# Turning gathered embedding rows on VectorE instead of TensorE, for five of sixteen groups, in a DLRM interaction kernel

## The chip, the cores and the metric

One core of a Trainium2 chip runs the whole kernel. The metric is the device time of one execution in microseconds, and the median over the runs counts.

## What is computed

The batch has 512 samples. For each sample the 26 embedding rows (128 float32 numbers each) of 26 tables and the dense row of 128 numbers are put together as 27 vectors; the 351 products of two different vectors follow, and then a tower of three layers:

```python
combined = jnp.concatenate([dense_features[:, None, :], sparse_features], axis=1)
interactions = jnp.einsum('bnd,bmd->bnm', combined, combined)
interactions_flat = interactions[:, _TRIU_I, _TRIU_J]
z = jnp.concatenate([dense_features, interactions_flat], axis=1)
h = jnp.concatenate([z, r_dense_features], axis=1)
h = jnp.maximum(h @ W_top1 + b_top1, 0.0)     # 607 -> 512
h = jnp.maximum(h @ W_top2 + b_top2, 0.0)     # 512 -> 256
y = h @ W_top3                                # 256 -> 1
```

All data is float32.

## The kernel before, in words

The features' buffer `xt` (line 140) holds the 27 vectors with the feature dimension on the partitions: partition d, then pair of samples, then vector, then sample within the pair. It is filled in three ways.

The dense vector is copied by ScalarE. Eleven small tables (1,000 rows) are not gathered. They are loaded whole, and `lookup` (line 314) multiplies them on TensorE with one-hot matrices that VectorE makes (`compare`, line 551). A table enters as a rounded high part, which ScalarE casts, and a low part, which VectorE subtracts (`make_low`, line 567). ScalarE copies the result from PSUM into `xt`. There are 13 lookups: tables 0 to 8 over the whole batch, tables 9 and 10 over one half of the batch each time. Lookups 11 and 12 serve the second half, and TensorE mixes them with the first products.

The other fifteen tables are gathered by GpSimd with indirect DMAs (line 307), one for each table and tile of 128 samples, so 60 in all. A gathered block `rows_sb` (line 139) has samples on the partitions and must be turned. The blocks are worked on in groups: each of the four tiles has four groups, of 4, 4, 4 and 3 blocks. So groups 0 to 3 belong to tile 0, 4 to 7 to tile 1, 8 to 11 to tile 2 and 12 to 15 to tile 3. `turn_group(g)` (line 340) transposes a group's blocks on TensorE into one of the two banks of `ps_rows`, and `copy_group(g)` (line 657) on ScalarE takes the bank to `xt`. `rows_sb` has room for two tiles, so the gathers of group g from 8 on wait until group g-8 has been turned (line 300).

Once all of a tile's vectors are in `xt`, `gram(t, quarter)` (line 353) makes 32 products of 27 by 27 numbers for each of its four quarters. On VectorE, `pack(t)` (line 583) transposes them from PSUM in blocks of 32 by 32 (line 589) and copies the upper triangle with nine copies (line 594) into `z`. `turn_z` on TensorE and `copy_z` on ScalarE turn `z` for layer 1 (`layer1_dense`, `layer1_pairs`), whose results go through `relu1_low` on ScalarE and `relu1_high` on VectorE (line 602) to `layer2`, `relu2` and `layer3`. The tiles are pipelined: TensorE puts the products of tile t+1 between the layer parts of tile t, in an order that is written out by hand (lines 471 to 542). The order on VectorE and ScalarE is written out too (lines 614 to 621 and 699 to 746). Each engine runs its own list in order and waits on semaphores.

At the places that matter here, TensorE runs (line 474) group 7 behind lookup 10, (line 484) group 8, `layer1_dense(0, ...)`, `turn_z(0)`, group 9, `gram(1, 0)`, the pairs of tile 0 with the rest of tile 1's products, `layer2(0, 0)`, `gram(1, 3)`, `layer2(0, 1)`, `layer1_dense(1, ...)`, (line 501) group 10, `turn_z(1)`, group 11 and `gram(2, 0)`. The same round follows for tile 1, with (line 517) group 12, `turn_z(2)`, group 13, `layer1_pairs(2, 0)`, group 14, group 15 and the products of tile 3. VectorE, after its work for the lookups, runs `pack(0)`, `relu1_high(0)`, `pack(1)`, `relu1_high(1)` and so on.

Of the kernel before, what the change touches and what calls it, by code (L numbers as in the profile page):

```python
# [15 lines left out]
P = 128  # L16
B = 512
D = 128
# [3 lines left out]
RUN = 2  # L22
TILES = B // P
# [38 lines left out]
ROWS_RING = 2  # L62
# [4 lines left out]
FIRST_HALF_UP_TO = NOH  # L67
# [3 lines left out]
FIRST_GATHERED = 1 + NOH  # L71
GROUP_SIZES = [4, 4, 4, 3]
GROUP_STARTS = [sum(GROUP_SIZES[:i]) for i in range(len(GROUP_SIZES))]
GROUPS = [(t, i, k) for t in range(TILES) for i, k in zip(GROUP_STARTS, GROUP_SIZES)]
assert sum(GROUP_SIZES) == len(GATHERED)

AFTER_LOOKUP = [[], [], [], [0], [1], [2], [3], [4], [5], [6], [7]]
LOOKED_UP_BESIDE = sum(len(gs) for gs in AFTER_LOOKUP)
assert sum(AFTER_LOOKUP, []) == list(range(LOOKED_UP_BESIDE)) and len(AFTER_LOOKUP) == FIRST_HALF_UP_TO
GROUPS_UP_TO = [sum(t <= tile for t, _, _ in GROUPS) for tile in range(TILES)]  # L80

WARM_UP = 13
GATHERS_PER_LOOKUP = 3
# [38 lines left out]
def build(nc, dense_by_column, ids, ids_by_table, tables, w1, w2, columns, identity, out):  # L122
    with ExitStack() as ctx:
        def sb(name, shape, dt):
            return ctx.enter_context(nc.sbuf_tensor(name, shape, dt))

        def sem(name):
            return ctx.enter_context(nc.semaphore(name))
# [10 lines left out]
        rows_sb = sb("rows_sb", [P, ROWS_RING, len(GATHERED), D], F32)  # L139
        xt = sb("xt", [P, B // RUN, N, RUN], F32)  # L140
# [21 lines left out]
        def bank(name, banks=1):  # L162
            return ctx.enter_context(nc.psum_tensor(name, [P, banks, BANK], F32))

        ps_a = bank("ps_a", 2)
        ps_rows = bank("ps_rows", 2)
# [14 lines left out]
        group_landed = [sem(f"group_landed{g}") for g in range(len(GROUPS))]  # L181
# [9 lines left out]
        lookup_copied = sem("lookup_copied")  # L191
        group_turned = sem("group_turned")
        group_copied = sem("group_copied")
        gram_done = sem("gram_done")
        blocks_turned = sem("blocks_turned")
        triangle_packed = sem("triangle_packed")
# [27 lines left out]
        def h1_block(t, m):  # L224

            return ps_a[:, m // 2, (m % 2) * P:(m % 2 + 1) * P]
# [61 lines left out]
        @block.gpsimd  # L288
        def _(pool):

            for c in SIZES:
                first = FIRST_COLUMN[c]
                pool.iota(row_id[:, first:first + c], [[1, c]], base=0, channel_multiplier=c,
                          allow_small_or_imprecise_dtypes=True).then_inc(row_id_ready, 1)
                pool.iota(row_id[:, first + c:first + c + 1], [[1, 1]], base=1 - c, channel_multiplier=-c,
                          allow_small_or_imprecise_dtypes=True).then_inc(row_id_ready, 1)
            pool.wait_ge(ids_landed, 16)
            for g, (t, first, n) in enumerate(GROUPS):
                if t >= ROWS_RING:
                    pool.wait_ge(group_turned, g - ROWS_RING * len(GROUP_SIZES) + 1)  # L300
                for k in range(first, first + n):
                    f = GATHERED[k]
                    issued = t * len(GATHERED) + k
                    if issued >= GATHERS_AHEAD and (issued - GATHERS_AHEAD) % GATHERS_PER_LOOKUP == 0:
                        lookups = (issued - GATHERS_AHEAD) // GATHERS_PER_LOOKUP + 1
                        pool.wait_ge(lookup_done, min(lookups, len(LOOKUPS)))
                    pool.indirect_dma_start(  # L307
                        rows_sb[:, t % ROWS_RING, k, :], None, tables[f],
                        bass.IndirectOffsetOnAxis(ids_sb[:, t, f:f + 1], 0),
                    ).then_inc(group_landed[g], 16)  # L310

        @block.tensor
        def _(pe):
# [26 lines left out]
            def turn_group(g):  # L340

                t, first, n = GROUPS[g]
                if g >= 2:
                    pe.wait_ge(group_copied, g - 1)
                if g == 0:
                    pe.wait_ge(ident_landed, 16)
                pe.wait_ge(group_landed[g], 16 * n)
                for slot in range(n):
                    last = pe.transpose(ps_rows[:, g % 2, slot * P:(slot + 1) * P],  # L349
                                        rows_sb[:, t % ROWS_RING, first + slot, :], ident)  # L350
                last.then_inc(group_turned, 1)

            def gram(t, quarter):

                half, first = divmod(quarter * SPQ, SPB)
                if quarter == 0:

                    pe.wait_ge(group_copied, GROUPS_UP_TO[t])  # L360
                    pe.wait_ge(lookup_copied, FIRST_HALF_UP_TO if t < TILES // 2 else len(LOOKUPS))
                    if t == 0:
                        pe.wait_ge(dense_copied, 1)
                        pe.wait_ge(gram_zeroed, 1)
                    else:
                        pe.wait_ge(blocks_turned, t)
                for s in range(first, first + SPQ):
                    for j in range(P // NPAD):
                        b = t * P + j * NPAD + half * SPB + s
                        x = xt[:, b // RUN, :, b % RUN]  # L370
                        last = pe.matmul(ps_gram[j * NPAD:j * NPAD + N, half, s * N:(s + 1) * N], x, x,  # L371
                                         start=True, stop=True)
                if quarter == QUARTERS - 1:
                    last.then_inc(gram_done, 1)
# [96 lines left out]
            for i in range(FIRST_HALF_UP_TO):  # L471
                lookup(i)
                for g in AFTER_LOOKUP[i]:
                    turn_group(g)
# [6 lines left out]
            gram(0, 3)  # L481
            lookup(FIRST_HALF_UP_TO + 1, [2, 3])

            turn_group(8)
            layer1_dense(0, 0)
            layer1_dense(0, 1)
            turn_z(0)
            turn_group(9)
            gram(1, 0)
            layer1_pairs(0, 0)  # L490
            layer1_pairs(0, 1)
# [6 lines left out]
            layer2(0, 1)  # L498
            layer1_dense(1, 0)
            layer1_dense(1, 1)  # L500
            turn_group(10)
            turn_z(1)
            turn_group(11)

# [9 lines left out]
            layer2(1, 1)  # L514
            layer1_dense(2, 0)
            layer1_dense(2, 1)
            turn_group(12)
            turn_z(2)
            turn_group(13)

# [24 lines left out]
        def _(dve):  # L545
# [37 lines left out]
            def pack(t):  # L583

                dve.wait_ge(gram_done, t + 1)
                if t:
                    dve.wait_ge(triangle_packed, t)
                blocks = ps_gram[:, :, 0:SPB * N].rearrange("p k (s m) -> p m k s", m=N)
                dve.transpose(zz[:, 0:N, :], blocks).then_inc(blocks_turned, 1)  # L589
                dve.wait_ge(blocks_turned, t + 1)  # L590
                if t:
                    dve.wait_ge(z_turned, t)
                for r, (i, length, at) in enumerate(TRIANGLE):
                    last = dve.tensor_copy(  # L594
                        z[:, at:at + TRI * length].rearrange("p (r l) -> p r l", r=TRI),
                        diagonal(i, length))
                    if t == TILES - 1 and r in CHUNK_ENDS:
                        last.then_inc(last_packed, 1)
                if t < TILES - 1:
                    last.then_inc(triangle_packed, 1)  # L600

            def relu1_high(t):

                dve.wait_ge(h1_done, 2 * (t + 1))
                if t == 0:
                    dve.wait_ge(layers_landed, 32)
                if t >= 2:
                    dve.wait_ge(h2_done, t - 1)
                for m in range(M1 // 2, M1):
                    last = dve.tensor_scalar(h1[:, t % 2, m, :], h1_block(t, m),  # L610
                                             b1_sb[:, m:m + 1], 0.0, ALU.add, ALU.max)
                last.then_inc(h1_high_ready, 1)

            pack(0)
            relu1_high(0)
            pack(1)
            relu1_high(1)
            pack(2)
            relu1_high(2)
# [4 lines left out]
        def _(act):  # L624
# [32 lines left out]
            def copy_group(g):  # L657
                t, first, n = GROUPS[g]
                slots = slice(FIRST_GATHERED + first, FIRST_GATHERED + first + n)
                act.wait_ge(group_turned, g + 1)  # L660
                act.copy(xt[:, t * P // RUN:(t + 1) * P // RUN, slots, :].rearrange("p q n r -> p n q r"),  # L661
                         ps_rows[:, g % 2, 0:n * P].rearrange("p (n q r) -> p n q r", n=n, r=RUN)).then_inc(group_copied, 1)

            def copy_z(t):
                act.wait_ge(z_turned, t + 1)
# [43 lines left out]
            for h in range(FIRST_HALF_UP_TO):  # L709
# [6 lines left out]
                if h == WORK_RING:  # L716
                    act.wait_ge(dense_landed, 16)
                    act.copy(xt[:, :, 0, :], dense_sb[:, :].rearrange("p (q r) -> p q r", r=RUN)).then_inc(dense_copied, 1)
                for g in AFTER_LOOKUP[h]:
                    copy_group(g)  # L720
            copy_lookup(FIRST_HALF_UP_TO)
            copy_lookup(FIRST_HALF_UP_TO + 1)
            copy_group(8)
            copy_z(0)
            copy_group(9)
            relu1_low(0)
            relu2(0)
            copy_group(10)
            copy_z(1)
            copy_group(11)  # L730
            relu1_low(1)
            relu2(1)
            copy_group(12)
            copy_z(2)
            copy_group(13)
            relu1_low(2)
# [41 lines left out]
```

## Time and profile before

| | us |
|---|---|
| median of 3 runs | 103.11 (102.64 to 103.51) |
| the profiled execution's own time | 103.07 |
| its span, first to last instruction | 101.2 |
| TensorE busy in it | 94.3 |
| VectorE busy in it | 52.8 |
| ScalarE busy in it | 48.3 |
| GpSimd busy in it | 60.6 |

The span is what the profile's times count from. The 1.9 us between it and the execution's own time lie before the first and after the last instruction. The granted TensorE clock was 1.0 over the whole span.

### The profile page before, as it was taken

To read this page: it belongs to the slowest core of one execution; us is meant where nothing else is said; L and a number is where in the kernel's file an instruction comes from. 1 tells how busy PE (TensorE), PEld (TensorE's weight loads), DVE (VectorE), ACT (ScalarE), POOL (GpSimd) and SP (SyncE) were. 2 spreads that over 40 slices of the span, in tenths; PEclk is the share of its full clock that TensorE was granted. 3 is DMA by queue.
4 is the path that set the end of the run, shared out by engine and by line. 5 is a ranking of instruction groups with operands and counts; after the bars stand their busy time and mean duration, and the time that the engine had idled before them with its cause. 6 is when DMAs were issued, how large, how long until landed. Compare 5 with 4: busy or idle time off the path is not lost.

```text
span 101.2 us, 3474 instructions
## 1 busy us (share of the span) xinstructions
PE 94.3 (93%) x1525; PEld 77.4 (77%) x1525; DVE 52.8 (52%) x116; ACT 48.3 (48%) x82; POOL 60.6 (60%) x66
## 2 busy tenths in 40 slices
PE   5999997999999999999997999997999989979990
PEld 2357665778888888899986898896898979977870
DVE  4599999999999989907000800243001801035200
ACT  2844998299399489565310342007020356005251
POOL 1488877777777777777777777777777730000000
PEclk9999999999999999999999999999999999999999
DMA  2899999999997999622222222212222220000000
GB/s 61 237 323 262 296 274 279 262 263 278 283 240 209 243 324 369 209 55 52 58 58 52 57 53 58 62 52 58 52 57 53 58 52 0 6 6 0 6 0 1
DMA packets 5365, 13.46 MB, mean 133 GB/s; under 512 B 1731, under 2 KB 1991, under 8 KB 5222
## 3 DMA queue, kind: packets, MB, share of 16 engines
q1 hardware_dynamic: 3260, 9.11, 31.0%
q0 software_dynamic: 1920, 3.94, 15.5%
q8 instruction: 12, 0.20, 0.8%
q10 hardware_dynamic: 170, 0.18, 0.6%
q14 instruction: 3, 0.02, 0.1%
HBM read 13.23 MB, written 0.00 MB: 131 GB/s over the span
## 4 chain that ended last, share of the span: by engine, by line
PE 71%; DVE 18%; DMA 3%; issue 3%; ACT 3%; DVEq 0%
PE ps_a L334 29%; PE ps_gram L371 12%; DVE onehot L562 12%; PE ps_a L420 9%; PE ps_rows L349 6%; PE ps_h L434 5%; DVE part_sb L571 4%; PE ps_a L410 3%; DMA idrow<-ids_by_table 3%; PE ps_a L397 3%; PE ps_rows L447 2%; DVE table_sb L589 1%; ACT xt L661 1%; PE ps_h L460 1%; DVE z L594 1%
## 5 line engine op out<-in xcount | busy, mean ns | idle before, releaser
L307 POOL DMA_INDIRECT rows_sb<-tbl,ids_sb x60 | 60.1, 1002 | 20.8 <-issue 16.8
L334 PE MATMUL ps_a<-onehot,part_sb 125*128 125x512 f32 (+1 forms) x208 | 45.2, 367 | 0.8 <-DVE part_sb L571 0.5
L334 PEld LDWEIGHTS ps_a<-onehot,part_sb 125*128 125x128 f32 x208 | 34.1, 188 | 8.6 <-DVE part_sb L571 2.4
L562 DVE TENSOR_SCALAR onehot<-idrow,row_id 125x1024 fp32r<-125x1024 int16 (+1 forms) x42 | 27.9, 717 | 2.2 <-DMA idrow<-ids_by_table 1.7
L571 DVE TENSOR_TENSOR part_sb<-table_sb,part_sb 125x512 fp32r<-125x512 f32 x22 | 14.4, 677 | 2.3 <-ACT part_sb L633 2.3
L654 ACT COPY xt<-ps_a 128x512 f32<-128x512 f32 (+1 forms) x13 | 7.4, 570 | 16.3 <-PE ps_a L334 16.3
L371 PE MATMUL ps_gram<-xt 128*27 128x27 f32 x1024 | 13.2, 195 | 2.0 <-issue 1.1
L371 PEld LDWEIGHTS ps_gram<-xt 128*27 128x27 f32 x1024 | 11.0, 108 | 4.6 <-issue 1.5
L610 DVE TENSOR_SCALAR table_sb<-ps_a,columns_sb 128x128 f32<-128x128 f32 x8 | 2.4, 347 | 20.9 <-PE ps_a L420 17.8
L589 DVE STREAM_TRANSPOSE table_sb<-ps_gram 128x864 f32<-128x864 f32 x4 | 4.3, 1083 | 16.7 <-issue 8.5
L633 ACT CAST part_sb<-table_sb 125x1024 fp32r<-125x1024 f32 (+1 forms) x12 | 11.6, 975 | 2.7 <-DMA table_sb<-tbl 2.7
L661 ACT COPY xt<-ps_rows 128x512 f32<-128x512 f32 (+1 forms) x16 | 9.8, 613 | 1.8 <-PE ps_rows L349 1.7
L420 PE MATMUL ps_a<-table_sb,w_sb 128*128 128x128 f32 x72 | 9.7, 283 | 0.3 <-ACT table_sb L668 0.3
L691 ACT ACTIVATE table_sb<-ps_h,columns_sb 128x128 f32<-128x128 f32 x6 | 1.9, 363 | 16.9 <-PE ps_h L434 16.9
L349 PE MATMUL ps_rows<-ident_sb,rows_sb 128*128 128x128 f32 x60 | 9.2, 272 | 0.0
L420 PEld LDWEIGHTS ps_a<-table_sb,w_sb 128*128 128x128 f32 x72 | 8.6, 192 | 0.7 <-ACT table_sb L668 0.5
L349 PEld LDWEIGHTS ps_rows<-ident_sb,rows_sb 128*128 128x128 f32 x60 | 7.2, 141 | 0.8
L434 PE MATMUL ps_h<-table_sb,w_sb 128*128 128x128 f32 x48 | 7.0, 288 | 0.0
L643 ACT ACTIVATE distance<-idrow,row_id 125x1024 f32<-125x1024 int16 (+1 forms) x6 | 6.5, 1078 | 0.4 <-DMA idrow<-ids_by_table 0.4
L468 PE MATMUL ps_z<-zeros 128*128 128x512 bf16 x13 | 5.2, 588 | 1.2 <-DVE zeros L546 1.2
L648 ACT ACTIVATE onehot<-distance 125x1024 fp32r<-125x1024 f32 (+1 forms) x6 | 5.9, 991 | 0.4
L684 ACT ACTIVATE table_sb<-ps_a,columns_sb 128x128 f32<-128x128 f32 x8 | 2.5, 364 | 7.4 <-PE ps_a L420 5.4
(35 smaller groups left out, 44.0 us busy)
## 6 DMA issues: line engine op xcount, KB each, us to landing
table_sb<-tbl SPq DMA_DIRECT2D x11, 448.0 KB
idrow<-ids_by_table SPq DMA_DIRECT2D x5, 256.0 KB, 5.7
w_sb<-w SPq DMA_DIRECT2D x1, 1280.0 KB, 8.2
rows_sb<-tbl,ids_sb POOLq DMA_INDIRECT x60, 3.6
table_sb<-tbl SPq DMA_DIRECT2D x10, 52.0 KB
w_sb<-w SPq DMA_DIRECT2D x1, 512.0 KB, 8.8
dense_sb<-dense_by_column SPq DMA_DIRECT2D x1, 256.0 KB, 7.7
idrow<-ids_by_table ACTq DMA_DIRECT2D x1, 128.0 KB, 2.9
```

What stands on the lines that cost most here:

```text
L307: pool.indirect_dma_start(rows_sb[:, t % ROWS_RING, k, :], None, tables[f], bass.IndirectOffsetOnAxis(ids_sb[:, t, f:f + 1], 0),).then_inc ...
L334: last = pe.matmul(ps_a[:, i % 2, a:b], parts_sb[part][:, w, c * D:(c + 1) * D], unit_onehot(u, c)[:, member, a:b], start=(part == HIGH an ...
L349: last = pe.transpose(ps_rows[:, g % 2, slot * P:(slot + 1) * P], rows_sb[:, t % ROWS_RING, first + slot, :], ident)
L371: last = pe.matmul(ps_gram[j * NPAD:j * NPAD + N, half, s * N:(s + 1) * N], x, x, start=True, stop=True)
L420: last = pe.matmul(h1_block(t, m), w1_sb[:, c, m * P:(m + 1) * P], zt[:, t % 2, c, :], start=False, stop=(c == ZC - 1), skip_group_check=True)
L434: last = pe.matmul(h2_block(t, m), w2_sb[:, k, m * P:(m + 1) * P], h1[:, t % 2, k, :], start=(k == 0 and m == 0), stop=(k == M1 - 1), skip ...
L562: dve.tensor_scalar(unit_onehot(u, c), idrow[0:VP, w, 0:n, :], row_id[0:VP, first + c:first + c + 1], None, ALU.is_equal).then_inc(onehot_ ...
L571: dve.tensor_tensor(parts_sb[LOW][:, w, columns], table_sb[0:VP, s, columns], parts_sb[HIGH][:, w, columns].bitcast(F32), ALU.subtract).th ...
L633: act.copy(parts_sb[HIGH][:, w, first:end], table_sb[0:VP, s, first:end]).then_inc(part_ready[HIGH], 1)
L643: act.activation(distance[:, 0:n, :], idrow[0:VP, w, 0:n, :], ACT.Abs, bias=row_id[0:VP, negated:negated + 1]) \
L654: act.copy(xt[:, a // RUN:b // RUN, 1 + h, :], ps_a[:, i % 2, a:b].rearrange("p (q r) -> p q r", r=RUN)).then_inc(lookup_copied, 1)
L661: act.copy(xt[:, t * P // RUN:(t + 1) * P // RUN, slots, :].rearrange("p q n r -> p n q r"), ps_rows[:, g % 2, 0:n * P].rearrange("p (n q ...
```

## The change

Groups 7, 8, 9, 10 and 12 are no longer turned by TensorE and copied by ScalarE. A new function on VectorE, `lay_group`, turns each group with 16 transposes: for each of four bands of 32 samples and each of four bands of 32 features, one instruction turns the group's 4 (or 3) blocks of 32 by 32 from `rows_sb` straight into `xt`. Groups 7 and 8 are laid ahead of `pack(0)`, groups 9 and 10 between `pack(0)` and `relu1_high(0)`, group 12 between `pack(1)` and `relu1_high(1)`. The remaining eleven groups keep their places. Their semaphore values and the choice of the `ps_rows` bank go by the place among the turned groups.

```diff
-AFTER_LOOKUP = [[], [], [], [0], [1], [2], [3], [4], [5], [6], [7]]
+AFTER_LOOKUP = [[], [], [], [0], [1], [2], [3], [4], [5], [6], []]
+LAID = [7, 8, 9, 10, 12]
+TURNED = [g for g in range(len(GROUPS)) if g not in LAID]
+TURNED_UP_TO = [sum(GROUPS[g][0] <= tile for g in TURNED) for tile in range(TILES)]
+LAID_UP_TO = [sum(GROUPS[g][0] <= tile for g in LAID) for tile in range(TILES)]
+BLOCK = 32
...
                 if t >= ROWS_RING:
-                    pool.wait_ge(group_turned, g - ROWS_RING * len(GROUP_SIZES) + 1)
+                    freed = g - ROWS_RING * len(GROUP_SIZES)
+                    if freed in LAID:
+                        pool.wait_ge(group_laid, LAID.index(freed) + 1)
+                    else:
+                        pool.wait_ge(group_turned, TURNED.index(freed) + 1)
...
-                    pe.wait_ge(group_copied, GROUPS_UP_TO[t])
+                    pe.wait_ge(group_copied, TURNED_UP_TO[t])
+                    if LAID_UP_TO[t]:
+                        pe.wait_ge(group_laid, LAID_UP_TO[t])
...
-            turn_group(8)
             layer1_dense(0, 0)
             layer1_dense(0, 1)
             turn_z(0)
-            turn_group(9)
             gram(1, 0)
...
-            turn_group(10)
             turn_z(1)
             turn_group(11)
...
-            turn_group(12)
             turn_z(2)
             turn_group(13)
...
+            def lay_group(g):
+
+                t, first, n = GROUPS[g]
+                slots = slice(FIRST_GATHERED + first, FIRST_GATHERED + first + n)
+                dve.wait_ge(group_landed[g], 16 * n)
+                for a in range(0, P, BLOCK):
+                    samples = slice((t * P + a) // RUN, (t * P + a + BLOCK) // RUN)
+                    for d in range(0, D, BLOCK):
+                        last = dve.transpose(
+                            xt[d:d + BLOCK, samples, slots, :].rearrange("p q n r -> p n q r"),
+                            rows_sb[a:a + BLOCK, t % ROWS_RING, first:first + n, d:d + BLOCK])
+                last.then_inc(group_laid, 1)
+
+            lay_group(7)
+            lay_group(8)
             pack(0)
+            lay_group(9)
+            lay_group(10)
             relu1_high(0)
             pack(1)
+            lay_group(12)
             relu1_high(1)
```

On ScalarE `copy_group(8)`, `(9)`, `(10)` and `(12)` go from the written-out list, and group 7's copy goes with `AFTER_LOOKUP`.

## Rows read from the trace of the kernel before

**Rows 1.** The page: busy time of each engine, share of the span and instructions.
```profile
PE 94.3 (93%) x1525; PEld 77.4 (77%) x1525; DVE 52.8 (52%) x116; ACT 48.3 (48%) x82; POOL 60.6 (60%) x66
```

**Rows 2.** The chain that ended last, in order of time: start us, us, what.
```profile
48.52 0.33 PE ps_rows L349 x3
...
57.08 0.44 PE ps_rows L349 x4
...
57.65 1.13 PE ps_a L410 x8
...
67.03 1.09 PE ps_h L434 x8
...
69.01 0.45 PE ps_rows L349 x4
...
69.49 0.61 ACT xt L661
...
70.47 0.41 ACT xt L661
...
70.92 0.72 PE ps_gram L371 x50
...
81.29 0.49 ACT table_sb L668
...
81.82 1.61 PE ps_a L420 x12
...
84.53 0.33 PE ps_rows L349 x3
```

**Rows 3.** VectorE's timeline from 40 us on: start us, us, instructions, idle before.
```profile
46.78 0.68 DVE L581 TENSOR_TENSOR w1d<-w_sb 128x512 f32<-128x512 f32 x1
...
55.97 1.08 DVE L589 STREAM_TRANSPOSE table_sb<-ps_gram 128x864 f32<-128x864 f32 x1 [8.51 <-issue]
57.09 1.02 DVE L594 COPY z<-table_sb 128x78 f32<-128x78 f32 x9
64.38 0.61 DVE L610 TENSOR_SCALAR table_sb<-ps_a,columns_sb 128x128 f32<-128x128 f32 x2 [6.27 <-PE ps_a L420]
67.08 1.08 DVE L589 STREAM_TRANSPOSE table_sb<-ps_gram 128x864 f32<-128x864 f32 x1 [2.09 <-PE ps_gram L371]
...
75.68 0.61 DVE L610 TENSOR_SCALAR table_sb<-ps_a,columns_sb 128x128 f32<-128x128 f32 x2 [6.46 <-PE ps_a L420]
```

**Rows 4.** Groups of VectorE's instructions by form: busy us, mean ns of one.
```profile
L571 DVE TENSOR_TENSOR part_sb<-table_sb,part_sb 125x512 fp32r<-125x512 f32 x22 | 14.4, 677 | 2.3 <-ACT part_sb L633 2.3
L589 DVE STREAM_TRANSPOSE table_sb<-ps_gram 128x864 f32<-128x864 f32 x4 | 4.3, 1083 | 16.7 <-issue 8.5 <-PE ps_gram L371 8.2
...
L610 DVE TENSOR_SCALAR table_sb<-ps_a,columns_sb 128x128 f32<-128x128 f32 x8 | 2.4, 347 | 20.9 <-PE ps_a L420 17.8 <-PE ps_a L397 3.1
L594 DVE COPY z<-table_sb 128x78 f32<-128x78 f32 x4 | 0.9, 235 | 0.1
L594 DVE COPY z<-table_sb 128x69 f32<-128x69 f32 x4 | 0.9, 215 | 0.0
...
L594 DVE COPY z<-table_sb 128x6 f32<-128x6 f32 x4 | 0.6, 149 | 0.0
```

**Rows 5.** GpSimd's timeline from 40 us on: five of its gathers, start us, us.
```profile
41.75 1.02 POOL L307 DMA_INDIRECT rows_sb<-tbl,ids_sb  x1 [0.30 <-issue]
...
48.58 0.94 POOL L307 DMA_INDIRECT rows_sb<-tbl,ids_sb  x1 [0.30 <-PE ps_a L334]
...
57.32 0.94 POOL L307 DMA_INDIRECT rows_sb<-tbl,ids_sb  x1 [0.30 <-PE ps_a L334]
58.57 0.94 POOL L307 DMA_INDIRECT rows_sb<-tbl,ids_sb  x1 [0.30 <-issue]
...
81.04 0.94 POOL L307 DMA_INDIRECT rows_sb<-tbl,ids_sb  x1 [0.30 <-issue]
```

**Rows 6.** The tile of gathered rows, 74 to 90 us: time from a gather's start to landing.
```profile
DMA to landing us min/median/max: 2.5/2.5/2.7
```

More of the change, by code:

```diff
@@ L75 @@
 assert sum(GROUP_SIZES) == len(GATHERED)
-AFTER_LOOKUP = [[], [], [], [0], [1], [2], [3], [4], [5], [6], [7]]
-LOOKED_UP_BESIDE = sum(len(gs) for gs in AFTER_LOOKUP)
-assert sum(AFTER_LOOKUP, []) == list(range(LOOKED_UP_BESIDE)) and len(AFTER_LOOKUP) == FIRST_HALF_UP_TO
-GROUPS_UP_TO = [sum(t <= tile for t, _, _ in GROUPS) for tile in range(TILES)]
+AFTER_LOOKUP = [[], [], [], [0], [1], [2], [3], [4], [5], [6], []]
+assert len(AFTER_LOOKUP) == FIRST_HALF_UP_TO
+LAID = [7, 8, 9, 10, 12]
[3 more added lines that the diff above has]
+BLOCK = 32
 WARM_UP = 13
@@ L193, in build @@
         group_copied = sem("group_copied")
+        group_laid = sem("group_laid")
         gram_done = sem("gram_done")
@@ L342, in turn_group @@
                 t, first, n = GROUPS[g]
-                if g >= 2:
-                    pe.wait_ge(group_copied, g - 1)
-                if g == 0:
+                place = TURNED.index(g)
+                if place >= 2:
+                    pe.wait_ge(group_copied, place - 1)
+                if place == 0:
                     pe.wait_ge(ident_landed, 16)
@@ L348, in turn_group @@
                 for slot in range(n):
-                    last = pe.transpose(ps_rows[:, g % 2, slot * P:(slot + 1) * P],
+                    last = pe.transpose(ps_rows[:, place % 2, slot * P:(slot + 1) * P],
                                         rows_sb[:, t % ROWS_RING, first + slot, :], ident)
@@ L659, in copy_group @@
                 slots = slice(FIRST_GATHERED + first, FIRST_GATHERED + first + n)
-                act.wait_ge(group_turned, g + 1)
+                place = TURNED.index(g)
+                act.wait_ge(group_turned, place + 1)
                 act.copy(xt[:, t * P // RUN:(t + 1) * P // RUN, slots, :].rearrange("p q n r -> p n q r"),
-                         ps_rows[:, g % 2, 0:n * P].rearrange("p (n q r) -> p n q r", n=n, r=RUN)).then_inc(group_copied, 1)
+                         ps_rows[:, place % 2, 0:n * P].rearrange("p (n q r) -> p n q r", n=n, r=RUN)).then_inc(group_copied, 1)
             def copy_z(t):
@@ L722, in _ @@
             copy_lookup(FIRST_HALF_UP_TO + 1)
-            copy_group(8)
             copy_z(0)
-            copy_group(9)
             relu1_low(0)
             relu2(0)
-            copy_group(10)
             copy_z(1)
@@ L732, in _ @@
             relu2(1)
-            copy_group(12)
             copy_z(2)
```

## The prediction

> **What bounds the kernel now.** I read the page first, then the chain that ended last, then VectorE's timeline, the groups of VectorE's instructions by form, and GpSimd's gathers with their landing. TensorE is busy for 94.3 of 101.2 us, VectorE for 52.8 [rows 1]. The chain is TensorE nearly throughout, and the turns of gathered groups stand in it one after another as pieces of 0.33 (three blocks) or 0.44 us (four blocks) [rows 2]. VectorE's work for the lookups ends at 47.46 us (46.78 + 0.68), and it is mostly idle behind that: 8.5 us ahead of `pack(0)`, 6.3 ahead of `relu1_high(0)`, 6.5 ahead of `relu1_high(1)` [rows 3]. So the change takes work from the engine that sets the end and puts it into gaps of an idle one. Whether it pays depends on whether the work fits into the gaps, because behind each gap VectorE has something to do that TensorE waits for.
>
> **What is removed.** TensorE loses 19 transposes in five pieces: 0.33 + 4 x 0.44 = 2.1 us of the chain [rows 2] (of the five, the rows show those of groups 7, 8 and 10; 9 stands at 59.11 and 12 at 80.30, as long as 8). Not all of it comes back, piece by piece:
> - Group 7 (48.52): 0.33 us, and all behind it moves up.
> - Group 8 (57.08): nothing. `layer1_dense` started at 57.65, 0.57 us behind the lookup's end. It waits for ScalarE's copy of that lookup, and the turn stood inside this wait [rows 2].
> - Group 9 (59.11): 0.44. Sum for `gram(1, 0)`, which starts behind the turn: 0.77.
> - Group 10 (69.01): `turn_z(1)` needs `pack(1)`, which starts when `gram(1, 3)` ends (67.03) and takes 2.14 from 67.08, until 69.22 [rows 2, 3], so the turn hid 0.2 of that wait. What gains is ScalarE's chain, copy 10 (at 69.49), copy of z, copy 11, `gram(2, 0)` at 70.92. Without copy 10, from the end of `pack` it needs turn of z 0.33, copy of z 0.49, copy 11 0.41 [rows 2] and hand-overs of about 0.12, 1.35 us in place of 70.92 - 69.22 = 1.70: a gain of 0.35.
> - Group 12 (80.30): the same pattern, but only the copy of z counts for `layer1_pairs(2, 0)` (81.82). 0.37.
>
> If VectorE's work were free, `layer1_pairs(2, 0)` would come 0.33 + 0.44 + 0.34 + 0.36 = 1.47 us sooner. A second limit stands behind it. GpSimd issues one gather after another, every 1.25 us, whatever TensorE does. The last starts at 81.04 and lands 2.5 later, at 83.54 [rows 5, 6]. TensorE turned its group 15 at 84.53 [rows 2] and would want to at 83.06. So at most 84.53 - 83.6 = 0.93 us of the gain gets through. The waits that free `rows_sb` cost nothing: group 15's gathers (from 78.5 on) now wait for group 7's laying, done some 25 us earlier.
>
> **What is added.** 80 VectorE transposes, 64 of 32 x 128 elements and 16 (group 7) of 32 x 96. The trace has no operation like it: its transposes are of 864 elements from PSUM, and every VectorE instruction in it works from partition 0 on. Two numbers are open.
>
> The duration of one. The PSUM transpose of 864 takes 1083 ns [rows 4]. At one element in 1.04 ns (the slope between the copies of 6 and 69 elements, and no transpose of 864 could be slower than that by much) 900 of it are elements and 183 fixed. The 512-element subtraction from SBUF has 677 - 533 = 144 fixed, the copy of 6 elements 143, the PSUM operation of 128 elements 347 - 133 = 214, so SBUF saves about 70 [rows 4]. For 128 elements (133 ns): 133 + 183 - 70 = 246 at least, 133 + 144 = 277 by the copies, 133 + 183 = 316 at most. I take 270, and 33 less for 96 elements.
>
> The distance from one start to the next. The nine copies of `pack` have durations that grow evenly from 149 to 235 ns, some 1.7 us in sum, but take 1.02 together [rows 3, 4]: each starts about 0.08 before its predecessor's end. That gives 270 - 75 = 195 ns. The other end is the pair in which the second must see the first finished: the transpose at 55.97 takes 1.083, and the copy starts at 57.09, 0.037 after its end [rows 3]. That gives up to 270 + 37 = 307. All nine copies read and write the same partitions as their predecessor. In `lay_group` the partitions written change with every instruction, those read with every fourth. I take the upper end less a part of the hand-over: 295 ns. No row shows such a pair, so 195 and, with the longest duration, 353 stay as ends.
>
> The Trainium skill, VectorE: DVE Perf Modes, section Two Vector instructions with no wait between them, speaks against the change: a Vector instruction whose output or input starts in another group of 32 partitions than its predecessor's starts only when every earlier one has finished. It calls this a model. By it the overlap of the copies is lost in all 80 instructions and the time is slower than before by the amount below; by the copies' row alone the change gains. No row here has such a pair.
>
> **The sum at 295 ns.** Four blocks take 16 x 0.295 = 4.72 us, three 16 x 0.262 = 4.19.
> - Group 7 is laid from 47.46 (end of line 581) [rows 3] to 51.65. It has landed: its gathers are issued before those of group 8, and group 8's last starts at 48.58 [rows 5].
> - Group 8 lands at about 51.2 and is laid until 56.37. The products of tile 0 end 0.33 sooner than the 55.97 less a hand-over of 0.05 at which `pack(0)` started [rows 3], at 55.6, so `pack(0)` starts 0.8 late against that, at 56.41, and ends at 58.55 (2.14 long). `turn_z(0)` would come at 58.45: TensorE loses 0.15. `gram(1, 0)` starts 0.6 sooner than before.
> - Groups 9 and 10 (10's last gather starts at 58.57, lands at 61.1 [rows 5]) are laid from 58.55 to 67.99. `relu1_high(0)` stands behind them. Before, it started at 64.38 as soon as its input was there [rows 3], which would now be at 63.8. It lasts 0.61 and now ends at 68.65, hand-over included. TensorE wants `layer2(0, 1)` at 67.03 - 0.6 = 66.4, which needs it, and waits until 68.68. **This is the step that decides.** The 0.6 gained has become 1.65 lost.
> - `pack(1)` follows at 68.68 and ends at 70.82; with 1.35 to `gram(2, 0)` that is 72.17, before 70.92: 1.25 late.
> - Group 12 is laid from 70.8 to 75.5, and `relu1_high(1)` has its input at 75.64 + 1.25 = 76.9 [rows 3]: hidden, with 1.3 us to spare.
> - In the next round 0.37 comes back: `layer1_pairs(2, 0)` 0.88 late. The last gather, landed at 83.54, is then early enough, and the rest is as before.
>
> 0.9 us slower: a span of 102.1 and, on the profiled execution's own 103.07, 103.97. That execution lies 0.04 under the median. Forecast **104.0 us**. The end moves by 4 x 16 = 64 ns for each ns of the distance, less where lay 8 ends before the products: 0.281 us is break-even with before, 0.313 gives 2.0 more than before (105.1), 0.27 gives 0.7 less.
>
> **The rivals.**
> - *The transposes overlap* as the copies do: 195 ns. Four blocks take 3.1 us, three 2.6. Lay 8 ends at 54.3, lays 9 and 10 go from 57.8 to 64.1, and `relu1_high(0)` is done at 64.7, before the 66.26 at which TensorE wants it. All five fit. The gain of 1.47 is cut to 0.93 by the last gather: 102.1 us. For it: the copies' row, and gaps of 8.5 and 6.3 us for 5.7 and 6.3 us of work. Against it: those copies never change partitions. It decides below some 244 ns.
> - *They are longer still*, 320 ns: durations near 290 with the hand-over of 0.037. Lay 8 ends at 57.2, `pack(0)` at 59.35, lays 9 and 10 at 69.6, `relu1_high(0)` at 70.3, `pack(1)` at 72.4, `gram(2, 0)` 2.85 late, the end 2.5 late: 105.6. At 353 it would be above 107. For it: the fixed part of the only transpose, 183. Against: it reads PSUM.
> - *GpSimd is slowed.* The gather at 41.75, while VectorE and the loads were busy, took 1.02 us, the later ones 0.94 [rows 5]. If laying does that, 15 us of it cover 12 gathers at 195 ns, 1.0 us; the last lands at 84.5, and the first rival's gain is gone: 103.1. At 295 ns TensorE comes to group 15 only at 85.4, and the delay is hidden. Against it: the gather at 57.32, beside `pack(0)`'s copies, took 0.94 as well [rows 3, 5].
>
> **How the numbers follow.** The forecast's case (280 to 313 ns, 103.1 to 105.1) 0.40; overlap (102.1) 0.34; longer (105.1 to 107) 0.20; slowed gathers with overlap (103.1) 0.06. A measurement of this kernel tells about 1% from no change. Faster by over 1% means under 102.08, which is where the overlap case lies, so half of it: 0.17. Slower by over 1% is above 104.14: half of the forecast's case and all of the longer one, 0.40. The rest is 0.43. The range is 102.0 to 106.0. It leaves out the longest durations above and a little of the overlap case below.
>
> **What would show it.** Right, if two successive laying transposes start 0.28 to 0.31 us apart, if VectorE has no gap between `pack(0)` and `relu1_high(0)`, if TensorE sits idle for some 2 us ahead of line 434's second half of tile 0 with line 610 as releaser, and if `gram(2, 0)` starts near 72. Wrong, if the distance is about 0.2, if that wait is absent, and if TensorE instead waits ahead of group 15 for the gathers' DMA.

## The result, and the profile after

The changed kernel takes 106.36 us (median of four, 105.48 to 107.91), before 103.31. The ratio is 1.0265, with a 95% interval of 1.0208 to 1.0321: slower by 2 to 3%. Ratios, here and below, leave out executions that took over 1.5% longer than the fastest of the same kernel, here the longest of the four. The forecast was 104.0, the range ended at 106.0. The execution profiled is that longest one, 107.91 us with a span of 106.1: TensorE's granted clock was at its lower level for nearly 7 us in it (its mean over the span was 0.968). In the other three the mean granted clock was 1.0 and the spans were 103.7 to 104.7.

The page of the changed kernel, busy times and two rows of the 40 slices, which answer to [rows 1]:

```profile
PE 94.3 (89%) x1506; PEld 77.9 (73%) x1506; DVE 76.3 (72%) x196; ACT 45.9 (43%) x77; POOL 60.8 (57%) x66
...
DVE  3799999999999799289999999999902520216100
...
PEclk9999999999999999999999999955699999999999
```

VectorE is now busy for 76.3 us in place of 52.8, with hardly a gap between 47 and 77 us. TensorE lost 19 transposes and is still busy for 94.3, since some of its work ran at the lower clock (in the run with nearly free laying, below, the same 1506 multiplications take 92.9 at a clock of 1.0).

VectorE's timeline, changed kernel (start us, us, instructions), against [rows 3]:

```profile
47.29 9.67 DVE L629 STREAM_TRANSPOSE xt<-rows_sb 32x96 f32<-32x96 f32 x32
56.99 1.08 DVE L596 STREAM_TRANSPOSE table_sb<-ps_gram 128x864 f32<-128x864 f32 x1
58.11 1.02 DVE L601 COPY z<-table_sb 128x78 f32<-128x78 f32 x9
59.05 10.18 DVE L629 STREAM_TRANSPOSE xt<-rows_sb 32x128 f32<-32x128 f32 x32
69.26 0.61 DVE L617 TENSOR_SCALAR table_sb<-ps_a,columns_sb 128x128 f32<-128x128 f32 x2
69.79 1.07 DVE L596 STREAM_TRANSPOSE table_sb<-ps_gram 128x864 f32<-128x864 f32 x1
70.89 1.02 DVE L601 COPY z<-table_sb 128x78 f32<-128x78 f32 x9
71.83 5.05 DVE L629 STREAM_TRANSPOSE xt<-rows_sb 32x128 f32<-32x128 f32 x16
```

Groups 9 and 10 take 10.18 us (16 transposes each, 0.318 us from start to start) in a gap that was 6.27 long. `relu1_high(0)` (line 617) starts at 69.26 in place of 64.38 and `pack(1)` (line 596) at 69.79 in place of 67.08, each without a pause behind the work ahead of it: VectorE itself is late, no longer waiting for TensorE.

TensorE's timeline, changed kernel, around that point:

```profile
66.33 0.75 PE L382 MATMUL ps_gram<-xt 128*27 128x27 f32 x64
69.93 2.07 PE L445 MATMUL ps_h<-table_sb,w_sb 128*128 128x128 f32 x8 [2.85 <-DVE table_sb L617]
71.79 1.91 PE L421 MATMUL ps_a<-dense_sb,w1d 128*128 128x128 f32 x8
73.50 0.85 PE L393 MATMUL ps_z<-ident_sb,z 128*128 128x128 f32 x3
74.14 0.85 PE L358 MATMUL ps_rows<-ident_sb,rows_sb 128*128 128x128 f32 x3
75.57 0.91 PE L382 MATMUL ps_gram<-xt 128*27 128x27 f32 x64 [0.59 <-ACT xt L687]
```

`gram(1, 3)` ends near 67.0. The second half of `layer2(0)` then waits 2.85 us for line 617, the wait that the prediction named. The eight multiplications behind it take 2.07 us in place of 1.09 on the chain, and the turn of z starts only at 73.50, though `pack(1)` was done at 71.91. The page's clock row shows 5, 5, 6 in the slices from 69.0 us to 76.9. `gram(2, 0)` starts at 75.57 in place of 70.92.

### The profile page after: what moved, and what is told of

It is laid out like the page before. It is cut to its first block, busy times and chain, and to the rows that moved or that the text cites. A ratio compares the mean times of both kernels' runs of the same rounds, so it can differ in the third digit from the quotient of the medians.

```text
span 106.1 us, 3509 instructions
## 1 busy us (share of the span) xinstructions
PE 94.3 (89%) x1506; PEld 77.9 (73%) x1506; DVE 76.3 (72%) x196; ACT 45.9 (43%) x77; POOL 60.8 (57%) x66
## 4 chain that ended last, share of the span: by engine, by line
PE 51%; DVE 30%; DMA 7%; issue 5%; ACT 4%; SPq 1%
PE ps_a L342 24%; DVE xt L629 17%; PE ps_gram L382 6%; PE ps_a L431 6%; DMA table_sb<-tbl 5%; PE ps_h L445 4%; DVE onehot L569 4%; PE ps_rows L358 3%; DVE table_sb L596 3%; DVE z L601 3%; PE ps_a L408 3%; DVE part_sb L578 2%; DMA idrow<-ids_by_table 2%; PE ps_a L421 2%; ACT part_sb L658 2%
## 5 line engine op out<-in xcount | busy, mean ns | idle before, releaser
L342 PE MATMUL ps_a<-onehot,part_sb 125*128 125x512 f32 (+1 forms) x208 | 44.6, 365 | 1.5 <-ACT part_sb L658 0.8
L629 DVE STREAM_TRANSPOSE xt<-rows_sb 32x128 f32<-32x128 f32 (+1 forms) x80 | 23.8, 298 | 1.1
L445 PE MATMUL ps_h<-table_sb,w_sb 128*128 128x128 f32 x48 | 7.9, 313 | 2.9 <-DVE table_sb L617 2.9
L445 PEld LDWEIGHTS ps_h<-table_sb,w_sb 128*128 128x128 f32 x48 | 6.6, 214 | 3.1 <-DVE table_sb L617 3.0
L687 ACT COPY xt<-ps_rows 128x512 f32<-128x512 f32 (+1 forms) x11 | 6.8, 617 | 0.5 <-PE ps_rows L358 0.5
L358 PE MATMUL ps_rows<-ident_sb,rows_sb 128*128 128x128 f32 x41 | 6.6, 283 | 0.0
L358 PEld LDWEIGHTS ps_rows<-ident_sb,rows_sb 128*128 128x128 f32 x41 | 5.3, 147 | 0.8
```

The lines of the kernel that those rows point to most:

```text
L342: last = pe.matmul(ps_a[:, i % 2, a:b], parts_sb[part][:, w, c * D:(c + 1) * D], unit_onehot(u, c)[:, member, a:b], start=(part == HIGH an ...
L358: last = pe.transpose(ps_rows[:, place % 2, slot * P:(slot + 1) * P], rows_sb[:, t % ROWS_RING, first + slot, :], ident)
L445: last = pe.matmul(h2_block(t, m), w2_sb[:, k, m * P:(m + 1) * P], h1[:, t % 2, k, :], start=(k == 0 and m == 0), stop=(k == M1 - 1), skip ...
L629: last = dve.transpose(xt[d:d + BLOCK, samples, slots, :].rearrange("p q n r -> p n q r"), rows_sb[a:a + BLOCK, t % ROWS_RING, first:first ...
```

## The experiments

All are compared with runs of the kernel before on the same chip. Where an experiment leaves out work of the kernel, the text says what.

**The changed kernel again** (no edit).

> The changed kernel once more. My theory: laying transposes start 0.318 us apart, so line 617's first pair (relu1_high of tile 0) ends near 69.9 and TensorE waits some 2.9 us ahead of the second half of layer2 of tile 0. With the clock at 1.0 throughout this costs 2.5 us over the kernel before: 105.6 us. Rival A: the drop of TensorE's clock to half that the first profile shows right behind this wait (68 to 75 us) belongs to the change and comes in every execution: then this profile shows it at the same place again and the time is near 108. Rival B: it comes in some executions only: then the granted clock here is 1.0.

Measured: 106.92 us, 1.035 times before [1.030, 1.041]. In its profile line 617's pair ends at 69.88, TensorE waits 2.85 us, and the clock drops again. Its stretches (us; length; busy time of PE, PEld, DVE, ACT, POOL; granted clock; DMA):

```profile
68.00:70.00 2.00, 0.06 (x1) 0.07 (x1) 1.93 (x7) 0.00 (x0) 1.39 (x3) 1.00 0.11 33
70.00:72.00 2.00, 2.00 (x11) 2.00 (x12) 1.97 (x11) 0.34 (x2) 1.64 (x2) 0.60 0.26 66
72.00:74.00 2.00, 2.00 (x12) 2.00 (x11) 1.92 (x7) 0.30 (x3) 1.45 (x2) 0.55 0.19 49
```

From 70 to 74 us the clock is at its lower level for most of the time, right behind the stretch in which TensorE was idle. Rival B holds in part: of the eight executions of this kernel so far, four had a mean granted clock of 1.0 and took 105.5 to 106.5 us, four had 0.97 to 0.98 and took 106.9 to 107.9. The ratio 1.035 holds three of these four, the ratio 1.0265 none of them.

**Distances by pattern.** Left out: the laid features (they stay zero, here and in the next two experiments); 80 instructions of the same size write a spare buffer, `scratch`, in the patterns told below. VectorE clears the laid places of `xt` once, ahead of 46 us.

```diff
-                for a in range(0, P, BLOCK):
-                    samples = slice((t * P + a) // RUN, (t * P + a + BLOCK) // RUN)
-                    for d in range(0, D, BLOCK):
-                        last = dve.transpose(
-                            xt[d:d + BLOCK, samples, slots, :].rearrange("p q n r -> p n q r"),
-                            rows_sb[a:a + BLOCK, t % ROWS_RING, first:first + n, d:d + BLOCK])
+                if g > 7:
+                    dve.wait_ge(group_laid, LAID.index(g))
+                for k in range(16):
+                    d = k % 4 * BLOCK
+                    source, target = {7: (0, 0), 8: (0, d), 9: (d, 0), 10: (64, 64), 12: (0, d)}[g]
+                    last = (dve.tensor_copy if g == 12 else dve.transpose)(
+                        scratch[target:target + BLOCK, k, 0:n, :],
+                        rows_sb[source:source + BLOCK, t % ROWS_RING, first:first + n, d:d + BLOCK])
```

> One look at distances, a pattern for each group, all into a spare buffer: group 7 reads partitions 0 to 31 and writes 0 to 31; group 8 reads the same and writes others each time; group 9 reads others each time and writes the same; group 10 reads and writes 64 to 95; group 12 is tensor_copy in place of transpose, reading the same and writing others each time. My theory: 0.20 us for group 7 (96 elements), 0.23 for group 10, 0.32 for groups 8 and 9 (a change on either side is enough), and group 12's copies lose their overlap as well: as far apart as they are long. Rival (transposes never overlap): 0.285, 0.32, 0.32, 0.32, and the copies overlap by 0.07 as those of pack do.

Measured: the transposes' durations (ns, min/median/max) for groups 7, 8, 9 and 10, from the line's own view in four stretches:

```profile
L636 DVE STREAM_TRANSPOSE scratch<-rows_sb x16: 223/224/259, 47.7 to 50.1; 32x96 f32<-32x96 f32 x16
...
L636 DVE STREAM_TRANSPOSE scratch<-rows_sb x16: 299/302/304, 51.5 to 56.3; 32x128 f32<-32x128 f32 x16
...
L636 DVE STREAM_TRANSPOSE scratch<-rows_sb x16: 289/299/307, 58.7 to 63.4; 32x128 f32<-32x128 f32 x16
...
L636 DVE STREAM_TRANSPOSE scratch<-rows_sb x16: 259/260/302, 63.8 to 66.7; 32x128 f32<-32x128 f32 x16
```

Group 10 (reads and writes partitions 64 to 95 all the time) has 0.260 long transposes; those of groups 8 (only the written partitions change) and 9 (only the read ones) are 0.30 long. The first two of group 8 on the chain of waits:

```profile
51.54 0.30 DVE scratch L636
51.84 0.01 issue
51.86 0.30 DVE scratch L636
```

They start 0.315 us apart, 0.013 behind the predecessor's end. With fixed partitions the sixteen of group 7 take 2.65 us, so (2.65 - 0.22) / 15 = 0.162 apart. The copies of group 12, with the written partitions changing, take 3.96 us of busy time in 4.16: no overlap, while `pack`'s copies, which stay on their partitions, overlap. So the change of partitions takes the overlap away, a change on one side is enough, and it happens to copies too (a change of the read side alone was tried only with transposes). It also lengthens the transpose by 0.04, for which no run shows a reason. In the changed kernel the transposes of four blocks last 0.304, as long as here, so the layout of `xt` into which they write adds nothing.

That an instruction which starts in other partitions than the one before it, on either side, waits until that one has finished is stated by the Trainium skill (VectorE: DVE Perf Modes, Two Vector instructions with no wait between them). The trace agrees: 0.013 us behind the predecessor's end with a change, 0.062 ahead of it without (group 7: 0.224 long, 0.162 apart).

**Same partitions for all.** As above, but:

```diff
-                    source, target = {7: (0, 0), 8: (0, d), 9: (d, 0), 10: (64, 64), 12: (0, d)}[g]
-                    last = (dve.tensor_copy if g == 12 else dve.transpose)(
+                    source, target = 0, 0
+                    last = dve.transpose(
```

> All 80 transposes stay, at their size, but all read partitions 0 to 31 and write partitions 0 to 31 of a spare buffer (the laid features stay zero). My theory, that the distance is long because each transpose writes to other partitions than the one before it: each now starts about 0.07 us before its predecessor's end, 0.23 us apart, groups 9 and 10 are done near 65.5, TensorE's wait is gone and the time is 102.2 to 102.6. Rival: transposes never overlap, whatever partitions they write: 0.32 us apart and 105.6 or more, as with the change.

Measured: 103.65 us, 1.003 times before [0.999, 1.007]. VectorE's timeline, groups 8, 9 and 10 and `relu1_high(0)`:

```profile
51.21 3.19 DVE L636 STREAM_TRANSPOSE scratch<-rows_sb 32x128 f32<-32x128 f32 x16 [1.11 <-DMA rows_sb<-tbl,ids_sb]
...
57.71 3.18 DVE L636 STREAM_TRANSPOSE scratch<-rows_sb 32x128 f32<-32x128 f32 x16
61.18 3.19 DVE L636 STREAM_TRANSPOSE scratch<-rows_sb 32x128 f32<-32x128 f32 x16 [0.28 <-DMA rows_sb<-tbl,ids_sb]
64.31 0.56 DVE L622 TENSOR_SCALAR table_sb<-ps_a,columns_sb 128x128 f32<-128x128 f32 x2
```

(3.19 - 0.26) / 15 = 0.195 us apart, and `relu1_high(0)` is done at 64.9. The same number and size of transposes, without changes of partitions, costs about 3% less: the whole loss hangs on the length and the distance of the transposes. But nothing is won against before either. The expected 102.2 to 102.6 did not come.

**Nearly free laying.** The same once more, with one of the 16 transposes of each group left in:

```diff
-                for k in range(16):
+                for k in range(1):
```

> The changed kernel with one of the 16 transposes of each laid group left in (into a spare buffer; those features stay zero), so that VectorE's work is nearly free. If the gains and the gathers' limit were worked out rightly, TensorE comes to layer1_pairs of tile 2 about 1.5 us sooner than before, then waits ahead of group 15 for gathers that land at 83.5, and the time is 0.9 us below the kernel before: 102.2. If the gathers are no limit, 101.7. If the removed turns were hidden anyway, no change: 103.1.

Measured: 103.82 us, 1.003 [0.999, 1.008]. So 2.1 us less of TensorE's work, with next to nothing added on VectorE, is worth nothing; 1.47 had been counted. TensorE started `layer1_pairs(2, 0)` at 81.91, before at 81.82, and did not wait for group 15's gathers: the second limit was never reached. TensorE's own waits from 48 to 92 us in the two traces (us in total, times, longest), first before, then this one:

```profile
PE ps_gram L371 <- issue: 1.1, 2, 0.6
PE ps_gram L371 <- ACT xt L661: 0.8, 1, 0.8
PE ps_a L420 <- ACT table_sb L668: 0.3, 1, 0.3
```

```profile
PE ps_gram L383 <- issue: 1.7, 3, 0.6
PE ps_z L394 <- DVE z L606: 0.8, 2, 0.5
PE ps_gram L383 <- ACT xt L694: 0.6, 1, 0.6
PE ps_a L422 <- ACT xt L686: 0.6, 1, 0.6
```

TensorE stood for 3.7 us in place of 2.2, 1.5 us more. Of this, 0.8 are waits for VectorE's `pack` ahead of `turn_z(1)` and `turn_z(2)`, and 0.6 for ScalarE's copy of a lookup ahead of `layer1_dense(0, 0)`; before, turns of groups stood in these places. Another 0.6 are pauses ahead of the small products in which it waited for nothing that the profile shows; its waits for ScalarE's other copies were 0.5 shorter. (The 2.7 and 4.0 us of the expectations below come from a view that adds up the pauses of the multiplications and those of the weight loads, which run beside them; TensorE's multiplications alone have 1.1 and 1.7.) Behind the end of `pack(1)` at 69.28, the chain of this trace runs:

```profile
69.33 0.56 PE ps_z L394 x3
69.89 0.02 issue
69.91 0.48 ACT table_sb L701
70.39 0.41 ACT xt L694
70.80 0.04 issue
```

The turn of z takes 0.56 us in it, where the prediction had 0.33, so from the end of `pack(1)` to `gram(2, 0)` at 70.84 it is 1.56 us, not 1.35.

**Group 10 back on TensorE and ScalarE.**

```diff
-LAID = [7, 8, 9, 10, 12]
+LAID = [7, 8, 9, 12]
...
-            lay_group(10)
...
+            turn_group(10)
             turn_z(1)
...
+            copy_group(10)
             copy_z(1)
```

> The changed kernel with group 10 alone back on TensorE and ScalarE. If the step that decides is relu1_high(0) and pack(1) standing behind the laying of two groups, this takes off nearly all of the loss: group 9 is laid by 64.3, relu1_high(0) starts as soon as its input is there, no wait of TensorE at layer2, no drop of the clock, and the time is 103.0 to 103.6. If the loss were spread over all laid groups (a fifth each), 105.8.

Measured: 103.80 us, 1.0076 [1.0038, 1.0114], just above the 103.0 to 103.6 that were expected. VectorE's timeline:

```profile
59.38 5.06 DVE L630 STREAM_TRANSPOSE xt<-rows_sb 32x128 f32<-32x128 f32 x16
64.75 0.61 DVE L618 TENSOR_SCALAR table_sb<-ps_a,columns_sb 128x128 f32<-128x128 f32 x2 [0.32 <-PE ps_a L431]
```

At this point VectorE waits for TensorE again (0.32 us), not the other way round. One group of five carries over 2 of the 3 us. Group 8 is the likely source of the 0.8% that is left: its laying ends at 57.29, 1.8 us after the products of tile 0, and TensorE waits 1.19 us for `pack(0)` ahead of `turn_z(0)`. The next run, without group 8's laying, bears that out.

**Groups 8 and 10 back**, one group in each of VectorE's gaps: the same edit for both:

```diff
-LAID = [7, 8, 9, 10, 12]
+LAID = [7, 9, 12]
```

> Groups 7, 9 and 12 are laid by VectorE, 8 and 10 go back to TensorE and ScalarE: one group for each of VectorE's gaps. All of it fits at 0.32 us a transpose, so TensorE's wait of 2.9 us and the clock's drop behind it are gone. TensorE has 1.2 us less to do. By the removed work alone: 0.9 to 1.1 us faster than before, 102.2. By what the look with nearly free laying showed (the removed 2.1 us came back as nothing, and the products of tiles 1 and 2 had more idle time put down to issue, 4.0 us in place of 2.7): no change, 103.1 to 103.4, with more such idle time than before's 2.7.

Measured: 102.94 us against 103.25, 0.9957 [0.9920, 0.9994]. That is 0.4% for 1.2 us less work on TensorE, at the edge of what these runs can tell from no change; the removed work alone was expected to give 102.2. VectorE's timeline, then TensorE's:

```profile
58.01 5.05 DVE L631 STREAM_TRANSPOSE xt<-rows_sb 32x128 f32<-32x128 f32 x16
63.89 0.61 DVE L619 TENSOR_SCALAR table_sb<-ps_a,columns_sb 128x128 f32<-128x128 f32 x2 [0.82 <-PE ps_a L431]
```

```profile
73.95 0.25 PE L382 MATMUL ps_gram<-xt 128*27 128x27 f32 x4 [0.39 <-issue]
...
89.66 1.00 PE L382 MATMUL ps_gram<-xt 128*27 128x27 f32 x94 [0.95 <-issue]
```

The laying ends 0.8 us ahead of `relu1_high(0)`'s input. Pauses put down to issue stand inside runs of products: 1.7 us of TensorE's own time from 48 to 92 us, as with the nearly free laying.

**TensorE's wait filled, 24 multiplications.** `busy(n)` makes n float32 multiplications of the identity by itself, 128 columns, into columns that nothing reads.

```diff
             gram(1, 3)
+            busy(24)
             layer2(0, 1)
```

> The changed kernel with 24 float32 multiplications of 128 columns (2.6 us, into unused columns of a bank) where TensorE waits for relu1_high(0). Theory: the clock falls because TensorE sits idle for 2.85 us there. Then with the fill the granted clock stays at 1.0 from 68 to 76 us, gram(2, 0) starts at 73.3 in place of 74.9 to 75.6, and the time is 105.3 to 105.6, against 106.9 for the changed kernel. Rival: the drop has nothing to do with this wait: it stays, and the time stays at 106.9 or goes up.

Measured: 108.47 us, 1.048 [1.039, 1.057]. The clock stayed at 1.0, but the fill took 5.62 us: a float32 multiplication of 128 columns is two passes of 0.11 us, where a float32 transpose is one. TensorE came 2.6 us late out of its own fill (72.72, where line 617's pair, here line 625, was done at 70.1). So the expected 105.3 to 105.6 did not come. The size was a mistake of mine, and the next run has half.

**The same with `busy(12)`.**

> The changed kernel with 12 float32 multiplications of 128 columns where TensorE waits for relu1_high(0). The run with 24 showed that one lasts 0.22 us, not 0.11, so that its fill was 5.6 us and held TensorE up by 2.6; 12 last 2.6 us, inside the wait of 2.85. Theory (the clock falls because TensorE sits idle there): granted clock 1.0 from 68 to 76 us, layer2's second half at 70.1, gram(2, 0) at 73.4, and a time of 105.4 to 106.0, against 106.9 for the changed kernel. Rival (the drop is not from this wait): it stays and the time stays near 106.9.

Measured: 106.64 us, 1.033 [1.028, 1.037]. Its stretches:

```profile
68.00:70.00 2.00, 2.00 (x20) 2.00 (x19) 1.90 (x7) 0.00 (x0) 1.70 (x2) 1.00 0.26 66
70.00:72.00 2.00, 2.00 (x18) 1.82 (x18) 1.97 (x7) 0.29 (x2) 1.39 (x3) 1.00 0.21 53
72.00:74.00 2.00, 1.44 (x12) 1.02 (x10) 1.93 (x12) 1.19 (x4) 1.45 (x2) 1.00 0.21 53
```

With TensorE kept busy the clock stays at 1.0, and `gram(2, 0)` starts at 74.08, against 74.92 and 75.57 in the two profiles without a fill. In this execution `layer2`'s second half was 0.6 later than in those (70.52); VectorE's laying had started 0.55 later (47.84), long before the fill. So like for like it is 1.4 and 2.1 sooner. The mean granted clock was 0.997 or more in all eight executions with a fill (24 or 12), against four of eight at 0.97 to 0.98 without; no execution of a kernel without this wait was below 0.996. So the drop is tied to the idle wait, as far as eight against eight can show it. The time did not come down to the expected 105.4 to 106.0: 106.64 is 0.3 under the second measurement of the changed kernel, but 0.3 over the first, and above the 105.5 to 106.5 of its executions without a drop. The drop is not what makes the kernel slower than before.

**Longer instructions ahead of every quarter, on the kernel before.**

```diff
+                busy(2)
                 for s in range(first, first + SPQ):
```

> The kernel before with two more float32 multiplications of 128 columns (0.22 us) ahead of the products in each of the 16 quarters: 3.5 us more work for TensorE in 32 instructions. Theory: the small products run at the pace at which TensorE's instructions are supplied, and every long instruction ahead of them lets the supply get ahead, so that removing turns gave nothing and adding long instructions costs less than they last: 0.5 to 2.3 us more. Rival: TensorE's own work sets the pace throughout: 3.5 us more, 106.7.

Measured: 109.49 us, 1.060 [1.052, 1.067]. By the size just told, the added work was 64 passes of 0.11 us, 7.0 us and not 3.5. Of these 6.2 showed. No idle time put down to issue is left ahead of the products (before: 1.1), which fits the theory that long instructions let the supply get ahead. But they buy back less than 1 us of their 7: the rival, by which TensorE's own work sets the pace, is the nearer one, and the 0.5 to 2.3 of the theory was too low even in proportion.

**Nearly free laying again, and with TensorE's time put back** (0.44 us at each of the five places of the removed turns; here into bank 1 of `ps_rows`). `busy` is another function here: it always makes two multiplications, and its argument is the number of group copies that must be done, which they long are.

```diff
+                if i == FIRST_HALF_UP_TO - 1:
+                    busy(6)
...
+            busy(7)
             layer1_dense(0, 0)
             layer1_dense(0, 1)
             turn_z(0)
+            busy(7)
...
+            busy(7)
             turn_z(1)
...
+            busy(8)
             turn_z(2)
```

> The kernel with nearly free laying once more, beside the next one. Again no measurable difference from before: 103.2 to 103.8, and about 4.0 us of idle time ahead of the products put down to issue (before: 2.7).

> The kernel with nearly free laying (1.003 times before, measured twice), and at each of the five places where a group's turn was, two float32 multiplications of 128 columns into a bank that is free there (0.44 us, 2.2 us in all, 10 instructions in place of 19): TensorE has the removed time back, ScalarE and VectorE do not have the copies. Theory A: the removed 2.1 us are given back by waits for TensorE's own instructions, so that putting work back costs little: 1.003 to 1.007 of before, and the idle time put down to issue ahead of the products falls from 4.0 to near 3 us. Theory B: the kernel with nearly free laying carries some other cost of its own which hides a real gain of about 1.2 us: then this one is that much slower, 1.013 to 1.017.

Measured: nearly free laying, 103.59 us, 1.003 [1.000, 1.006]; TensorE's own idle time for issue ahead of the products was 1.8 us. With the work put back, 104.12 us (102.5 to 105.1) against 103.99 for before on that chip. Its runs scatter: only two of the six count in the ratio, 0.990 [0.982, 0.998], and the two medians have the ratio 1.001. TensorE's waits in the profile with the work put back, from 48 to 94 us:

```profile
PE ps_gram L389 <- issue: 1.0, 1, 1.0
PE ps_gram L389 <- ACT xt L706: 0.6, 1, 0.6
```

TensorE stands for 1.6 us in place of 3.7: the waits for `pack` and for the lookup's copy are gone, and the pauses for issue are down to 1.0. From the first product to the last it takes 40.7 us (50.5 to 91.2), as with the nearly free laying (49.5 to 90.2); before it took 40.3. Four of the five places lie in this stretch. So the work put back lay inside waits, and in the profiles it cost nothing. Neither theory's range was met: Theory B (a cost of its own that hides a gain) expected 1.3 to 1.7% over before, Theory A 0.3 to 0.7%. The profiles speak for A. With this scatter the times alone settle little, though both numbers above lie under B's range. How TensorE's instructions are supplied, and why the pauses stand where they do, was not tried.

## Why the prediction was wrong

**The deciding step was right in its mechanism, two terms of the sum were wrong in size.** The step marked as deciding is the one that decided: `relu1_high(0)` and `pack(1)` behind two laid groups, TensorE waiting 2.85 us with line 617 as releaser, `gram(2, 0)` late. Group 12 was hidden, and GpSimd was not slowed: from 48 us on its gathers took 0.94 to 0.95 us beside the laying, before 0.94; the one that began at 47.16 took 1.02, as its counterpart before. With group 10 alone put back, over 2 of the 3 us go.

**The distance, 0.295 us, measured 0.318.** The term mis-sized is the duration: 0.270 taken, 0.304 measured. The estimate came from fixed parts of instructions that stay on their partitions, and for those it was near (0.260). A change of partitions also makes the instruction itself longer, by 0.04. The hand-over was small, 0.014. "The end moves by 64 ns for each ns" was in the text: 0.023 more is 1.5 us by it. `relu1_high(0)` ended at 69.87, forecast 68.65, and `pack(1)` at 71.91, forecast 70.82: 1.1 us for the sum. The rival at 320 ns described this kernel, with 105.6; it had 0.20 and the forecast's case 0.40. No row put 0.295 ahead of it, and at 64 ns per ns the two sides of 0.313 called for more equal chances.

**The clock.** Nothing in the prediction looked at what TensorE does behind a wait of 2 us. In the profiled execution `gram(2, 0)` came 5.64 us behind the start of `layer2`'s second half (69.93 to 75.57), with the fill of 12 and the clock at 1.0 it came 3.56 behind it (70.52 to 74.08). So 2.1 us are the lower clock. In the three other executions the mean clock was 1.0, so this explains the longest execution, not the median.

**The gain of the removed turns, 1.47 us, measured none.** "If VectorE's work were free, `layer1_pairs(2, 0)` would come 1.47 us sooner": with the nearly free laying it came 0.1 later (81.91). On the way, forecast against measured, `gram(1, 0)` came 0.77 and 0.52 us sooner, `layer2(0, 1)` 0.77 and 0.18 (66.78 in place of 66.96), `gram(2, 0)` 1.1 and 0.08, and from there to `layer1_pairs(2, 0)` nothing came back. Two causes are seen. TensorE's removed work was replaced by waits and pauses, 1.5 us of them, a pause of 0.49 us inside the products ahead of `layer2(0, 0)` among them; the prediction took each turn at its full 0.33 or 0.44 us, as if removal were gain. And the 0.35 and 0.37 of groups 10 and 12 rested on 1.35 us from `pack` to the next products, in which the turn of z stood at 0.33; it takes 0.56 on the chain and the whole 1.56, so 0.2 of each gain was never there. (The sum in the text also writes 0.34 and 0.36 for these two, a slip of 0.02.) Why the pauses for issue grew is open.

The overlap rival was wrong for the same reason: 103.65 measured, 102.1 forecast. In the changed kernel too the 0.37 us did not come back in the round of tile 1: from `gram(2, 0)` to `layer1_pairs(2, 0)` it took 11.02 us, before 10.90. So 0.5 us too little there, and 0.2 between `pack(1)` and `gram(2, 0)`.

Together, for the profiled execution: 0.9 forecast + 1.1 distance + 2.1 clock + 0.7 gain = 4.8, and its span grew by 106.1 - 101.2 = 4.9. Without the clock it is 2.7, or 106.0 on before's 103.3; the executions without a drop took 105.5 to 106.5. The sum was fitted to this one trace, and its parts are good to 0.1 or 0.2.

## What to carry to other kernels

Work that moves into an idle engine's gap is paid for by the next thing in that engine's order: compare its length with the gap, and where the end moves many ns for each ns of an unknown duration, do not favour one side of the threshold without a row. Fill each gap to less than its length: three of five groups took 0.4% less than before, where five took about 3% more. And test a removal's worth by itself (the work left out, nothing put in its place) before building what is to replace it; here that run would have shown a ceiling of nothing.

## What the runs showed of the hardware that was not expected

- VectorE, float32 from SBUF, 32 partitions: a transpose of 32 x 128 is 0.260 us long and 0.195 from the next one if neither the read nor the written partitions change; 0.30 long and 0.315 apart if either does. A plain copy loses its overlap too when its written partitions change (16 in 4.16 us, 3.96 of it busy).
- TensorE's granted clock fell to half behind an idle stretch of 2.85 us in both profiles of the changed kernel, for 4 to 7 us. By the mean clock it fell in four of its eight executions, and in none of eight when the stretch was filled with work.
- A float32 multiplication of 128 columns took 0.22 us, a float32 transpose of the same size 0.11.
- TensorE's idle time ahead of many small multiplications, released by nothing that the profile shows, grew from 1.1 to 1.7 and 1.8 us (two profiles) when 19 longer instructions were taken out, was 1.0 when 10 were put back, and was gone with 32 added. One profile each stands behind the other numbers, and the cause is open.
